# A grouped convolution as products over summed weights: a stage's products issued between the next stage's sums

## The chip, the cores and the metric

The kernel runs on one core of a Trainium2 chip. The metric is the device time of one execution in microseconds. The kernel before took 949.01 us, the median of 3 runs (947.08 to 950.08).

## The reference

The input x has 2 samples of 512 channels by 256 positions. Four residual layers follow each other, each on a layer-normalised x: a block-sparse causal convolution, a mixture of experts, an attention, and the mixture of experts again. The change touches the convolution alone:

```
xb = x.reshape(batch, n_block_row, bs, t)                # 8 blocks of 64 channels
x_unfold = xb[:, cols].reshape(batch, n_blocks * bs, t)   # 128 weight blocks choose an input block
W = block_values.reshape(n_blocks * bs, bs, ks)           # 64 x 64 weights, 16 taps each
o = conv_general_dilated(x_unfold, W, (1,), [(ks - 1, 0)], feature_group_count=n_blocks)
y = zeros(...).at[:, rows].add(o)                         # and an output block
```

Columns and rows are drawn from 0 to 3 here (block_values was made for 256 channels), while x has 8 blocks.

## The kernel before

Weight blocks with the same pair of input block (column) and output block (row) act on the same data, so the kernel first **sums** them into 64 pair sums and then makes the **products** of the sums with the input. Two taps make a stage, eight stages (0 to 7) make the 16 taps.

For stages 0 to 4 (`NPE = 5`) TensorE makes the sums: the 128 weight blocks lie on the partitions, `onehot` (128 by 64) marks each block's pair, and 8 matmuls of 64 columns (line 481) fill a PSUM **bank**; a stage has 8 banks, and 4 banks are used in turn. ScalarE copies each bank, rounded, into `cv_ws_hi` (line 245), and VectorE writes the remainder into `cv_ws_lo` (line 334). A bank can be summed anew when the remainder of the bank four before is written. For stages 5 to 7 (`ND = 3`) VectorE makes the sums itself: 16 chunks `cv_shared` of 8 weight blocks each, fetched by GpSimd's queue (line 308, three buffers, called raw_d), are added block by block into `cv_acc` (line 360, 16 additions a chunk, whose places come from registers that `load_pairs` fills). When all 16 chunks are in, `cv_acc` is split for each of these stages in four pieces (lines 254 and 343).

The input is normalised into xn, which lies in the first part of the same buffer as raw_d, and is split into `cv_xc_hi` (line 237, ScalarE) and `cv_xc_lo` (line 384, VectorE), four pairs of operations each. The products of a stage are 24 matmuls of 512 columns (line 490: 8 pairs of blocks by hi*hi, hi*lo, lo*hi), which accumulate in four other banks over all stages. Other pairs are skipped by a branch. After a stage's products a tiny matmul on zeros (line 506) frees one of the two slots of split weights (`ws_free`).

The order on every engine is written out by hand, and each engine takes its instructions in that order. On TensorE: sums 0, sums 1, then products 0, sums 2, products 1, sums 3, products 2, sums 4, and products 3 to 7. The sync engine's queue fetches the weights of the sums in chunks of 1 MB (two banks each, three buffers) and, after the first three chunks, the input. What follows the convolution starts from its last products and is unchanged.

Of the kernel before, what the change touches and what calls it, by code (L numbers as in the profile page):

```python
# [146 lines left out]
def conv_phase(nc, cm, pm, ps, ins, following, prefetch):  # L147


    with ExitStack() as ctx:  # L150
# [7 lines left out]
        raw_d = [shared[:, i * DB * DROW:(i + 1) * DB * DROW].rearrange("p (n f) -> p n f", n=DB) for i in range(3)]  # L158
# [20 lines left out]
            "x_in", "zeros_ready", "ones_ready", "cr_in", "line_in", "iota_done", "const_done",  # L179
# [4 lines left out]
        raw_in = [cm(f"cv_raw_in{i}") for i in range(3)]  # L184
        raw_d_in = [cm(f"cv_raw_d_in{i}") for i in range(3)]
# [9 lines left out]
        ZEROED = 8  # L195
        PW = NW // PIECES
# [11 lines left out]
        def _(sp):  # L208
# [12 lines left out]
            sp.dma_start(line[:, 1, :], ins["rows"].rearrange("(a n) -> a n", a=1)).then_inc(s["line_in"], 16)  # L221
            blocks_first(2)
            sp.dma_start(X[:].rearrange("p n t -> p (n t)"), ins["x_tiles"]).then_inc(s["x_in"], 16)
# [5 lines left out]
        def _(a):  # L229
# [42 lines left out]
            round_banks(0, range(6, 7))  # L272
            round_input(1, 0)
            round_banks(0, range(7, 8))
            round_input(1, 1)
            round_banks(1)
# [6 lines left out]
        def _(g):  # L283
# [20 lines left out]
            g.wait_ge(s["xc_lo_done"], 4 * B)  # L304
            for d in range(NDC):
                if d >= 3:
                    g.wait_ge(s["added"], 2 + 2 * DB * (d - 2))
                g.dma_start(raw_d[d % 3], ins["wtaps"][d].rearrange("p (n f) -> p n f", n=DB)).then_inc(raw_d_in[d % 3], 16)
# [3 lines left out]
        def _(v):  # L312
# [49 lines left out]
            def statistics(b):  # L362
                for n in range(b * GC, (b + 1) * GC):
# [23 lines left out]
            v.wait_ge(s["x_in"], 16)  # L387
            statistics(0)
            variances(0)
            low_banks(0, range(2, 3))  # L390
            statistics(1)
            variances(1)
            low_banks(0, range(3, 4))
# [5 lines left out]
            normalize(0)  # L399
            low_banks(0, range(4, 5))  # L400
            normalize(1)
            low_banks(0, range(5, 7))
            split_input(0, 0)
            low_banks(0, range(7, 8))
            split_input(0, 1)
            low_banks(1, range(0, 1))
            split_input(1, 0)
            low_banks(1, range(1, 2))
            split_input(1, 1)
            low_banks(1, range(2, 5))  # L410
# [3 lines left out]
            pairs = load_pairs(0)  # L414
            low_banks(1, range(5, 6))
            add_blocks(0, pairs)
            low_banks(1, range(6, 7))
            pairs = load_pairs(1)
            low_banks(1, range(7, 8))
            more = load_pairs(2)  # L420
            add_blocks(1, pairs)
# [1195 lines left out]
```

## Time and profile before

| what | us |
|---|---|
| median of 3 runs | 949.01 |
| lowest and highest | 947.08 and 950.08 |
| the profiled execution | 945.27 |
| its span | 943.5 |
| its mean granted clock of TensorE, as a share of 2.4 GHz | 0.978 |
| last product of the convolution ends (idle matmuls of line 58 follow) | 147.53 |

The profile is of one execution. Its times count from the start of the span; the table's own time of that execution is 1.8 us longer than the span. The granted clock is 1.00 at 2.4 GHz and 0.50 at 1.2 GHz. An idle time in brackets stands before the instruction, with what ended it. Engines are PE (TensorE), PEld (its weight loads), DVE (VectorE), ACT (ScalarE), POOL (GpSimd) and SP (sync). Each 64-column matmul of line 481 appears as two records in the trace, so a bank is 16 records.

### The profile page before, as it was taken

How to read it: one execution, taken by the hardware profiler on the slowest of the kernel's cores; microseconds unless marked ns; L12 is line 12 of the kernel's file. 1: busy time of each engine (PE TensorE's matmuls, PEld its weight loads, DVE VectorE, ACT ScalarE, POOL GpSimd, SP SyncE). 2: the span in 40 equal slices, each digit the busy share in tenths (PEclk: the TensorE clock that was granted, in tenths of full speed). 3: DMA queues.
4: the chain of work that ended last, by engine and by line, in shares of the span. 5: the costliest groups of instructions: out<-in, count | busy, mean ns of one | idle time of the engine just before them, and what ended most of it. 6: DMA issues, size and time to landing. Idle time of an engine off the chain costs nothing. (4 is left out here: it accounts for less than half of the span.)

```text
span 943.5 us, 16979 instructions
## 1 busy us (share of the span) xinstructions
PE 918.7 (97%) x5723; PEld 800.4 (85%) x5729; DVE 540.5 (57%) x1360; ACT 439.6 (47%) x952; POOL 306.9 (33%) x282
## 2 busy tenths in 40 slices
PE   9999998999999999899999999999999999999998
PEld 7999975888888887678988997898887888888887
DVE  4788875533333335678668858866875533333334
ACT  7521252534334333466656746654762534333342
POOL 1011001265555564321212112122101265555663
PEclk9598899999999999999999999999999999999999
DMA  8699601111111110200100000000001111111111
GB/s 309 221 335 374 248 2 35 46 39 44 50 50 50 50 35 15 92 23 1 35 1 22 0 33 22 0 0 0 1 1 34 34 37 47 50 50 50 48 36 61
DMA packets 23216, 60.96 MB, mean 65 GB/s; under 512 B 3138, under 2 KB 11012, under 8 KB 20612
## 3 DMA queue, kind: packets, MB, share of 16 engines
q1 hardware_dynamic: 20868, 47.80, 15.2%
q0 software_dynamic: 2304, 12.58, 3.6%
q8 instruction: 26, 0.43, 0.2%
q14 instruction: 18, 0.15, 0.0%
HBM read 59.33 MB, written 1.05 MB: 64 GB/s over the span
## 5 line engine op out<-in xcount | busy, mean ns | idle before, releaser
L809 DVE TENSOR_TENSOR f_h<-f_scaled,bank 128x512 f32<-128x512 f32 (+1 forms) x90 | 60.8, 676 | 183.6 <-POOL f_scaled L710 183.6
L710 POOL TENSOR_TENSOR f_scaled<-f_act,f_gate_rows 128x512 f32<-128x512 f32 (+1 forms) x90 | 113.5, 1262 | 135.5 <-ACT f_act L641 135.1
L899 PE MATMUL bank<-f_xt_hi,f_w_lo 128*128 128x512 f32 (+1 forms) x400 | 157.0, 393 | 0.0
L899 PE MATMUL bank<-f_xt_hi,f_w_hi 128*128 128x512 f32 (+1 forms) x400 | 156.8, 392 | 0.0
L648 ACT ACTIVATE f_h_hi<-f_h 128x512 fp32r<-128x512 f32 (+2 forms) x102 | 63.6, 624 | 184.1 <-DVE f_h L809 184.1
L899 PE MATMUL bank<-f_xt_lo,f_w_hi 128*128 128x512 f32 (+1 forms) x400 | 123.6, 390 | 0.0
L1078 ACT ACTIVATE at_prob<-bank,at_sbias,at_qrs 128x512 f32<-128x512 f32 (+3 forms) x128 | 77.6, 616 | 85.6 <-DVE at_sbias L1248 85.6
L916 PE MATMUL bank<-f_w_lo,f_h_hi 128*128 128x256 f32 (+1 forms) x400 | 113.2, 283 | 0.0
L916 PE MATMUL bank<-f_w_hi,f_h_lo 128*128 128x256 f32 (+1 forms) x400 | 113.1, 283 | 0.0
L916 PE MATMUL bank<-f_w_hi,f_h_hi 128*128 128x256 f32 (+1 forms) x400 | 113.1, 283 | 0.0
L818 DVE TENSOR_TENSOR f_h_lo<-f_h,f_h_hi 128x512 fp32r<-128x512 f32 (+2 forms) x102 | 70.1, 688 | 73.1 <-ACT f_h_hi L648 72.8
L1147 POOL TENSOR_TENSOR at_qrs<-at_qsum,minus_half 128x4 f32<-128x4 f32 x32 | 32.7, 1022 | 208.4 <-DVE at_qsum L1204 208.4
L481 PE MATMUL bank<-cv_onehot,cv_raw 128*128 128x64 f32 x640 | 87.8, 308 | 2.9 <-DVE cv_ws_lo L334 2.6
L481 PEld LDWEIGHTS bank<-cv_onehot,cv_raw 128*128 128x128 f32 x640 | 86.9, 224 | 3.5 <-issue 2.1
L899 PEld LDWEIGHTS bank<-f_xt_lo,f_w_hi 128*128 128x128 f32 (+1 forms) x400 | 74.6, 187 | 17.1 <-DVE f_xt_lo L112 0.5
L641 ACT ACTIVATE f_act<-bank 128x512 f32<-128x512 f32 (+2 forms) x102 | 59.9, 590 | 58.8 <-PE bank L899 58.7
L899 PEld LDWEIGHTS bank<-f_xt_hi,f_w_hi 128*128 128x128 f32 (+1 forms) x400 | 75.1, 188 | 13.6 <-issue 0.4
L899 PEld LDWEIGHTS bank<-f_xt_hi,f_w_lo 128*128 128x128 f32 (+1 forms) x400 | 75.1, 188 | 13.1
L916 PEld LDWEIGHTS bank<-f_w_hi,f_h_hi 128*128 128x128 f32 (+1 forms) x400 | 76.4, 191 | 3.9
L916 PEld LDWEIGHTS bank<-f_w_hi,f_h_lo 128*128 128x128 f32 (+1 forms) x400 | 76.4, 191 | 3.6
L916 PEld LDWEIGHTS bank<-f_w_lo,f_h_hi 128*128 128x128 f32 (+1 forms) x400 | 76.4, 191 | 0.0
L697 POOL TENSOR_TENSOR f_w_lo<-f_wraw,f_w_hi 128x512 fp32r<-128x512 f32 x48 | 62.1, 1294 | 37.1 <-ACT f_w_hi L627 37.1
(185 smaller groups left out, 1996.7 us busy)
## 6 DMA issues: line engine op xcount, KB each, us to landing
cv_raw<-in_wconv SPq DMA_DIRECT2D x19, 1024.0 KB, 7.3
cv_shared<-in_wtaps POOLq DMA_DIRECT2D x16, 768.0 KB, 7.2
f_wraw<-in_w SPq DMA_DIRECT2D x44, 256.0 KB, 2.7
f_wraw<-in_w SPq DMA_DIRECT2D x44, 128.0 KB, 2.5
at_wraw<-in_wqkv SPq DMA_DIRECT2D x3, 768.0 KB, 4.3
at_oraw<-in_wo SPq DMA_DIRECT2D x4, 512.0 KB, 3.6
cv_raw<-in_wconv SPq DMA_DIRECT2D x2, 512.0 KB, 4.7
X<-in_x_tiles SPq DMA_DIRECT2D x1, 1024.0 KB, 10.7
```

The lines of the kernel that those rows point to most:

```text
L481: m = t.matmul(ps[q % BANKS][:].rearrange("p (w o) -> p w o", o=OB)[:, :, o], raw[c % 3][:, w0:w0 + P], onehot[:], start=True, stop=True)
L641: a.activation(act[half][0:rows, cols], pg[half][0:rows, cols], ACT.Silu).then_inc(s["act_done"], 1)
L648: a.activation(h_hi[slot][0:rows, cols], h_f[half][0:rows, cols], ACT.Copy).then_inc(s["h_hi_done"], 1)
L697: g.tensor_tensor(w_lo[slot][:, 0:n], raw_views(m, slot, rows)[0], w_hi[slot][:, 0:n].bitcast(F32), ALU.subtract).then_inc(s["w13_lo_done" ...
L710: g.tensor_tensor(scaled[half][:, cols], act[half][:, cols], gate_rows[:, half * HALF + cols.start:half * HALF + cols.stop], ALU.mult).the ...
L809: v.tensor_tensor(h_f[half][0:rows, cols], src[half][0:rows, cols], pu[half][0:rows, cols], ALU.mult)\
L818: v.tensor_tensor(h_lo[slot][0:rows, cols], h_f[half][0:rows, cols], h_hi[slot][0:rows, cols].bitcast(F32), ALU.subtract).then_inc(s["h_lo ...
L899: mm = t.matmul(bank[half][0:rows, :], w, x, start=q == 0, stop=q == len(steps) - 1)
L916: mm = t.matmul(bank, h[hslot][0:rows, tok], w, start=first and q == 0 and j % 2 == 0, stop=last and q == 2, skip_group_check=True)
L1078: a.activation(prob[:, sl, POFF[j]:POFF[j + 1]], ps[bank][:, col:col + n], ACT.Exp, bias=sbias[:, sl, j:j + 1], scale=qrs[:, sl, j:j + 1], ...
L1147: p.tensor_tensor(qrs[:, u % 2, :], qsum[:, u % 2, :], pm["minus_half"][:, 0:NQ], ALU.pow)\
```

## The change

On TensorE the products of stage n now stand between the banks of the sums of stage n+1. In stage 1 the first five banks stand alone; after the fifth come a wait for stage 0's splits and for all of `cv_xc_lo`, then six products behind each of banks 5 to 8 (counted from one). In stages 2 to 4 three products stand behind each bank from the second to the seventh, and six behind the eighth. Stages 4 to 7 have their products after all sums, as stages 3 to 7 had before. The flag of the branch is loaded before the sums.

On the sync engine the input is fetched in two halves, the first ahead of the third weight chunk, each with a semaphore of its own. On VectorE the first half is normalised before the statistics of the second, and the splits of the input alternate with single banks. The chunks of VectorE's own sums are spread: one behind each pair of banks from stage 1's last on, and two (14 and 15) behind all banks; `load_pairs` for these two stands behind the additions of the chunk before. The first of them is fetched without waiting for `cv_xc_lo`, into the third of the buffer that xn does not use.

The core of the diff; `sum_blocks(st)`, which was a loop over a stage's banks, is now `sum_bank(st, q)` with the same body for one bank:

```diff
-        raw_d = [shared[:, i * DB * DROW:(i + 1) * DB * DROW].rearrange("p (n f) -> p n f", n=DB) for i in range(3)]
+        raw_d = [shared[:, i * DB * DROW:(i + 1) * DB * DROW].rearrange("p (n f) -> p n f", n=DB) for i in (2, 0, 1)]
...
+            def input_half(b):
+                part = slice(b * GC, (b + 1) * GC)
+                sp.dma_start(X[:, part, :].rearrange("p n t -> p (n t)"),
+                             ins["x_tiles"][:, b * GC * D:(b + 1) * GC * D]).then_inc(x_in[b], 16)
+
+            input_half(0)
             blocks_first(2)
-            sp.dma_start(X[:].rearrange("p n t -> p (n t)"), ins["x_tiles"]).then_inc(s["x_in"], 16)
+            input_half(1)
...
-            round_banks(0, range(6, 7))
+            round_banks(0, range(6, 8))
             round_input(1, 0)
-            round_banks(0, range(7, 8))
+            round_banks(1, range(0, 1))
             round_input(1, 1)
-            round_banks(1)
+            round_banks(1, range(1, 8))
...
@@ -301,8 +309,9 @@
                 g.tensor_tensor(rstd[:, part], var_eps[:, part], pm["minus_half"][:, part], ALU.pow)\
                  .then_inc(s["rstd_ready"], 1)
             g.wait_ge(s["rstd_ready"], B)
-            g.wait_ge(s["xc_lo_done"], 4 * B)
             for d in range(NDC):
+                if d == 1:
+                    g.wait_ge(s["xc_lo_done"], 4 * B)
                 if d >= 3:
...
             def statistics(b):
+                v.wait_ge(x_in[b], 16)
...
 
             low_banks(0, range(0, 2))
-            v.wait_ge(s["x_in"], 16)
             statistics(0)
             variances(0)
-            low_banks(0, range(2, 3))
+            low_banks(0, range(2, 4))
+            normalize(0)
+            low_banks(0, range(4, 5))
             statistics(1)
             variances(1)
-            low_banks(0, range(3, 4))
+            low_banks(0, range(5, 6))
             v.wait_ge(s["line_in"], 32)
             v.tensor_copy(line_f[:], line[:]).then_inc(s["cr_conv"], 1)
             v.wait_ge(s["cr_conv"], 3)
             v.scalar_tensor_tensor(out=line_pair[:], in0=line_f[:, 0, :], scalar=float(NCB), in1=line_f[:, 1, :],
                                    op0=ALU.mult, op1=ALU.add).then_inc(s["cr_conv"], 1)
-            normalize(0)
-            low_banks(0, range(4, 5))
             normalize(1)
-            low_banks(0, range(5, 7))
-            split_input(0, 0)
-            low_banks(0, range(7, 8))
-            split_input(0, 1)
-            low_banks(1, range(0, 1))
-            split_input(1, 0)
-            low_banks(1, range(1, 2))
-            split_input(1, 1)
-            low_banks(1, range(2, 5))
+            low_banks(0, range(6, 8))
+            for q in range(4):
+                split_input(q // 2, q % 2)
+                low_banks(1, range(q, q + 1))
             v.sem_inc(s["added"], 2)
             v.wait_ge(s["cr_conv"], 4)
             v.wait_ge(s["acc_zeroed"], ZEROED)
             pairs = load_pairs(0)
+            low_banks(1, range(4, 5))
+            add_blocks(0, pairs)
             low_banks(1, range(5, 6))
-            add_blocks(0, pairs)
+            pairs = load_pairs(1)
             low_banks(1, range(6, 7))
-            pairs = load_pairs(1)
+            add_blocks(1, pairs)
             low_banks(1, range(7, 8))
-            more = load_pairs(2)
-            add_blocks(1, pairs)
-            add_blocks(2, more)
-            d = 3
             for st in range(2, NPE):
-                for q in range(0, SB, 2):
-                    if d == NDC:
-                        low_banks(st, range(q, q + 2))
-                        continue
-                    low_banks(st, range(q, q + 1))
+                for i in range(4):
+                    d = 4 * (st - 2) + i + 2
+                    low_banks(st, range(2 * i, 2 * i + 1))
                     pairs = load_pairs(d)
-                    low_banks(st, range(q + 1, q + 2))
-                    if q == SB - 2 and d + 1 < NDC:
-                        more = load_pairs(d + 1)
-                        add_blocks(d, pairs)
-                        d += 1
-                        pairs = more
+                    low_banks(st, range(2 * i + 1, 2 * i + 2))
                     add_blocks(d, pairs)
-                    d += 1
+            for d in range(4 * (NPE - 2) + 2, NDC):
+                add_blocks(d, load_pairs(d))
...
-            def convolve(st):
-                t.wait_ge(s["ws_lo_done"], splits_before(st + 1) if st < NPE else splits_before(st) + PIECES // 2)
-                for c in range(NCB // 2):
-                    for r in range(GC // 2):
-                        products(st % 2, c, r, st * 2)
+            def finish_products(st):
                 t.wait_ge(s["ws_lo_done"], splits_before(st + 1))
                 high_products(st)
                 t.matmul(ps[4][:, 0:1], zeros[:, 0:P], zeros[:, 0:1], start=False, stop=False)\
...
+            def convolve(st):
+                t.wait_ge(s["ws_lo_done"], splits_before(st + 1) if st < NPE else splits_before(st) + PIECES // 2)
+                for c, r in LOW_PAIRS:
+                    products(st % 2, c, r, st * 2)
+                finish_products(st)
+
+            def sum_and_convolve(st, first):
+                n = 0
+                for q in range(SB):
+                    sum_bank(st, q)
+                    if q == first:
+                        t.wait_ge(s["ws_lo_done"], splits_before(st))
+                        t.wait_ge(s["xc_lo_done"], 4 * B)
+                    if q >= first:
+                        end = len(LOW_PAIRS) * (q - first + 1) // (SB - first)
+                        for c, r in LOW_PAIRS[n:end]:
+                            products((st - 1) % 2, c, r, (st - 1) * 2)
+                        n = end
+                finish_products(st - 1)
...
-            sum_blocks(0)
-            sum_blocks(1)
             flag = t.value_load(any_high[0:1, 0:1], min_val=0, max_val=1)
-            t.wait_ge(s["xc_lo_done"], 4 * B)
-            for st in range(NPE - 2):
-                convolve(st)
-                sum_blocks(st + 2)
-            for st in range(NPE - 2, NST - 1):
+            for q in range(SB):
+                sum_bank(0, q)
+            sum_and_convolve(1, 4)
+            for st in range(2, NPE):
+                sum_and_convolve(st, 1)
+            for st in range(NPE - 1, NST - 1):
                 convolve(st)
             convolve_last(NST - 1)
```

The start of TensorE's products, before: the rows follow 16 banks of sums (`cv_onehot` is the mark of the pairs, `cv_raw` the weights).

```order
L481 MATMUL bank<-cv_onehot,cv_raw 128x64 x128
L524 TENSOR_LOAD cv_any_high
L524 ISA x2
L490 MATMUL bank<-cv_xc_hi,cv_ws_hi 128x512
L490 MATMUL bank<-cv_xc_hi,cv_ws_lo 128x512
L490 MATMUL bank<-cv_xc_lo,cv_ws_hi 128x512
L490 MATMUL bank<-cv_xc_hi,cv_ws_hi 128x512
```

The same place now, up to the first bank behind products:

```order
L476 MATMUL bank<-cv_onehot,cv_raw 128x64 x104
L485 MATMUL bank<-cv_xc_hi,cv_ws_hi 128x512
L485 MATMUL bank<-cv_xc_hi,cv_ws_lo 128x512
L485 MATMUL bank<-cv_xc_lo,cv_ws_hi 128x512
L485 MATMUL bank<-cv_xc_hi,cv_ws_hi 128x512
L485 MATMUL bank<-cv_xc_hi,cv_ws_lo 128x512
L485 MATMUL bank<-cv_xc_lo,cv_ws_hi 128x512
L476 MATMUL bank<-cv_onehot,cv_raw 128x64 x8
```

The first products stand behind 13 banks instead of 16, ahead of the last three banks of stage 1.

TensorE where stage 2 begins, now (`zeros` is the tiny matmul that frees the slot of stage 0):

```order
L497 MATMUL bank<-zeros 128x1
L476 MATMUL bank<-cv_onehot,cv_raw 128x64 x16
L485 MATMUL bank<-cv_xc_hi,cv_ws_hi 128x512
L485 MATMUL bank<-cv_xc_hi,cv_ws_lo 128x512
L485 MATMUL bank<-cv_xc_lo,cv_ws_hi 128x512
L476 MATMUL bank<-cv_onehot,cv_raw 128x64 x8
```

Before, all 64 sums of stage 2 stood here in one row; now eight sums and three products alternate.

VectorE from the first two banks on, before (`cv_shared` written is xn):

```order
L334 TENSOR_TENSOR cv_ws_lo<-bank,cv_ws_hi 128x64x8 x2
L364 BN_STATS cv_stats<-X 128x6 x4
L369 BN_AGGR cv_moments<-cv_stats 128x2 x4
L372 TENSOR_SCALAR cv_var_eps<-cv_moments 128x4
L334 TENSOR_TENSOR cv_ws_lo<-bank,cv_ws_hi 128x64x8
L364 BN_STATS cv_stats<-X 128x6 x4
L369 BN_AGGR cv_moments<-cv_stats 128x2 x4
L372 TENSOR_SCALAR cv_var_eps<-cv_moments 128x4
L334 TENSOR_TENSOR cv_ws_lo<-bank,cv_ws_hi 128x64x8
L395 CAST cv_line_f<-cv_line 1x256
L397 SCALAR_TENSOR_TENSOR cv_line_pair<-cv_line_f 1x128
L377 TENSOR_SCALAR cv_shared<-X,cv_moments,cv_rstd 128x256 x4
```

And now:

```order
L343 TENSOR_TENSOR cv_ws_lo<-bank,cv_ws_hi 128x64x8 x2
L374 BN_STATS cv_stats<-X 128x6 x4
L379 BN_AGGR cv_moments<-cv_stats 128x2 x4
L382 TENSOR_SCALAR cv_var_eps<-cv_moments 128x4
L343 TENSOR_TENSOR cv_ws_lo<-bank,cv_ws_hi 128x64x8 x2
L387 TENSOR_SCALAR cv_shared<-X,cv_moments,cv_rstd 128x256 x4
L343 TENSOR_TENSOR cv_ws_lo<-bank,cv_ws_hi 128x64x8
L374 BN_STATS cv_stats<-X 128x6 x4
L379 BN_AGGR cv_moments<-cv_stats 128x2 x4
```

The first normalisation has moved ahead of the second half's statistics.

VectorE at the end of its own sums, before:

```order
L360 ISA
L360 TENSOR_TENSOR cv_acc<-cv_acc,cv_shared 128x96
L334 TENSOR_TENSOR cv_ws_lo<-bank,cv_ws_hi 128x64x8 x2
L343 TENSOR_TENSOR cv_ws_lo<-cv_acc,cv_ws_hi 128x1024 x12
```

And now, at the first of the two late chunks and at the end:

```order
L369 ISA
L369 TENSOR_TENSOR cv_acc<-cv_acc,cv_shared 128x96
L358 TENSOR_LOAD cv_line_pair
L369 ISA
L369 TENSOR_TENSOR cv_acc<-cv_acc,cv_shared 128x96
```

```order
L369 TENSOR_TENSOR cv_acc<-cv_acc,cv_shared 128x96
L369 ISA
L369 TENSOR_TENSOR cv_acc<-cv_acc,cv_shared 128x96
L352 TENSOR_TENSOR cv_ws_lo<-cv_acc,cv_ws_hi 128x1024 x12
```

The last chunks (a register load, then 16 additions) have moved behind the last bank's split.

## Rows read from the trace of the kernel before

**Rows 1.** The page, busy time of each engine over the span.
```profile
PE 918.7 (97%) x5723; PEld 800.4 (85%) x5729; DVE 540.5 (57%) x1360; ACT 439.6 (47%) x952; POOL 306.9 (33%) x282
```

**Rows 2.** Busy us of PE, PEld, DVE, ACT, POOL by stretch; PEclk, DMA share, GB/s.
```profile
28.00:48.00 20.00, 20.00 (x94) 20.00 (x95) 16.67 (x29) 7.75 (x12) 1.83 (x3) 0.50 0.62 225
48.00:51.00 3.00, 3.00 (x10) 2.52 (x10) 2.73 (x11) 0.60 (x1) 0.54 (x1) 0.50 1.00 416
...
86.00:99.00 13.00, 13.00 (x55) 12.42 (x56) 12.67 (x53) 2.39 (x4) 1.61 (x3) 0.50 0.94 359
```

**Rows 3.** Waits of TensorE from 0 to 150 us: total, times, longest.
```profile
PE bank L481 <- DVE cv_ws_lo L334: 2.6, 3, 1.0
...
PE bank L517 <- DVE cv_ws_lo L343: 0.7, 1, 0.7
```

**Rows 4.** Timeline of TensorE: start us, us, instruction, in brackets idle before.
```profile
7.66 10.83 PE L481 MATMUL bank<-cv_onehot,cv_raw 128*128 128x64 f32 x96
...
27.93 20.72 PE L481 MATMUL bank<-cv_onehot,cv_raw 128*128 128x64 f32 x96 [0.87 <-DVE cv_ws_lo L334]
48.40 0.77 PE L490 MATMUL bank<-cv_xc_hi,cv_ws_hi 128*128 128x512 f32 x1
...
51.49 0.39 PE L490 MATMUL bank<-cv_xc_hi,cv_ws_lo 128*128 128x512 f32 x1
...
55.49 14.48 PE L481 MATMUL bank<-cv_onehot,cv_raw 128*128 128x64 f32 x128
69.78 0.48 PE L490 MATMUL bank<-cv_xc_hi,cv_ws_hi 128*128 128x512 f32 x1
70.10 0.40 PE L490 MATMUL bank<-cv_xc_hi,cv_ws_lo 128*128 128x512 f32 x1
...
75.53 7.34 PE L481 MATMUL bank<-cv_onehot,cv_raw 128*128 128x64 f32 x64
83.88 12.35 PE L481 MATMUL bank<-cv_onehot,cv_raw 128*128 128x64 f32 x64 [1.01 <-DVE cv_ws_lo L334]
...
123.20 0.47 PE L490 MATMUL bank<-cv_xc_hi,cv_ws_hi 128*128 128x512 f32 x1
...
128.92 0.48 PE L490 MATMUL bank<-cv_xc_hi,cv_ws_hi 128*128 128x512 f32 x1
...
147.53 1.89 PE L58 MATMUL bank<-zeros 128*128 128x512 bf16 x8
```

**Rows 5.** Timeline of VectorE, with the same columns.
```profile
12.14 0.69 DVE L334 TENSOR_TENSOR cv_ws_lo<-bank,cv_ws_hi 128x512 fp32r<-128x512 f32 x1 [1.17 <-ACT cv_ws_hi L245]
14.90 1.41 DVE L364 BATCH_NORM_STATS2 cv_stats<-X 128x6 f32<-128x256 f32 x4 [2.06 <-DMA X<-in_x_tiles]
...
20.20 1.36 DVE L377 TENSOR_SCALAR cv_shared<-X,cv_moments,cv_rstd 128x256 f32<-128x256 f32 x4
...
30.91 2.48 DVE L384 TENSOR_TENSOR cv_xc_lo<-cv_shared,cv_xc_hi 64x1024 fp32r<-64x1024 f32 x2
...
37.24 2.48 DVE L384 TENSOR_TENSOR cv_xc_lo<-cv_shared,cv_xc_hi 64x1024 fp32r<-64x1024 f32 x2
...
75.20 3.23 DVE L360 TENSOR_TENSOR cv_acc<-cv_acc,cv_shared 128x96 f32 x16 [1.30 <-DMA cv_shared<-in_wtaps]
...
117.13 3.22 DVE L360 TENSOR_TENSOR cv_acc<-cv_acc,cv_shared 128x96 f32 x16
...
124.47 4.63 DVE L343 TENSOR_TENSOR cv_ws_lo<-cv_acc,cv_ws_hi 128x1024 fp32r<-128x1024 f32 x4 [2.91 <-ACT cv_ws_hi L254]
```

**Rows 6.** Timeline of ScalarE, with the same columns.
```profile
15.22 0.61 ACT L245 ACTIVATE cv_ws_hi<-bank 128x512 fp32r<-128x512 f32 x1
...
21.66 2.14 ACT L237 ACTIVATE cv_xc_hi<-cv_shared 64x1024 fp32r<-64x1024 f32 x2 [3.97 <-DVE cv_shared L377]
...
123.37 3.91 ACT L254 ACTIVATE cv_ws_hi<-cv_acc 128x1024 fp32r<-128x1024 f32 x4 [5.10 <-PE bank L506]
```

**Rows 7.** Register loads of line 349: ns min/median/max, first and last start.
```profile
L349 DVEq TENSOR_LOAD <-cv_line_pair x16: 593/598/854, 39.3 to 115.8; - x16
```

More of the change, by code:

```diff
@@ L178, in conv_phase @@
         s = {n: cm(f"cv_{n}") for n in (
-            "x_in", "zeros_ready", "ones_ready", "cr_in", "line_in", "iota_done", "const_done",
+            "zeros_ready", "ones_ready", "cr_in", "line_in", "iota_done", "const_done",
             "cr_conv", "pair_part", "pair_ready", "onehot_ready", "acc_zeroed", "added",
@@ L184, in conv_phase @@
         raw_in = [cm(f"cv_raw_in{i}") for i in range(3)]
+        x_in = [cm(f"cv_x_in{b}") for b in range(B)]
         raw_d_in = [cm(f"cv_raw_d_in{i}") for i in range(3)]
@@ L195, in conv_phase @@
         ZEROED = 8
+        LOW_PAIRS = [(c, r) for c in range(NCB // 2) for r in range(GC // 2)]
         PW = NW // PIECES
@@ L468, in _, with sum_bank @@
             t.sem_inc(s["ws_free"], 2)
-            def sum_blocks(st):
-                for q in range(SB):
-                    c, part = st * (BS // CO) + q // CB, q % CB
-                    if c > 0 and part == 0:
-                        t.wait_ge(raw_in[c % 3], 16 * (c // 3 + (c % 3 > 0)))
-                    if st * SB + q >= BANKS:
-                        t.wait_ge(s["ws_lo_done"], st * SB + q - BANKS + 1)
-                    if c == 0:
-                        t.wait_ge(first_in[part], 16)
-                    for o in range(OB):
-                        w0 = (part * OB + o) * P
-                        m = t.matmul(ps[q % BANKS][:].rearrange("p (w o) -> p w o", o=OB)[:, :, o],
-                                     raw[c % 3][:, w0:w0 + P], onehot[:], start=True, stop=True)
-                    m.then_inc(s["summed"], 1)
+            def sum_bank(st, q):
+                c, part = st * (BS // CO) + q // CB, q % CB
+                if c > 0 and part == 0:
+                    t.wait_ge(raw_in[c % 3], 16 * (c // 3 + (c % 3 > 0)))
+                if st * SB + q >= BANKS:
+                    t.wait_ge(s["ws_lo_done"], st * SB + q - BANKS + 1)
+                if c == 0:
+                    t.wait_ge(first_in[part], 16)
+                for o in range(OB):
+                    w0 = (part * OB + o) * P
+                    m = t.matmul(ps[q % BANKS][:].rearrange("p (w o) -> p w o", o=OB)[:, :, o],
+                                 raw[c % 3][:, w0:w0 + P], onehot[:], start=True, stop=True)
+                m.then_inc(s["summed"], 1)
             def products(slot, c, r, tap):
```

## The prediction

> **What bounds the kernel now.** The page comes first: TensorE is busy 97% of the span [rows 1], so a change inside the convolution must shorten TensorE's own time there, or lengthen it. Then TensorE's waits: the sums wait 2.6 us in three pieces for VectorE's splits, and the last stage 0.7 us [rows 3]. That is little. The stretches with the granted clock say more [rows 2]: from 28 to 48 us and from 86 to 99 us TensorE is full and has 0.50 of its clock, so it works at 1.2 GHz. In the timeline each of these stretches begins at a wait (0.87 us ahead of 27.93, 1.01 us ahead of 83.88) and consists of sums. At full clock a stage's 8 banks take 55.49 to 69.78, 14.3 us or 1.79 a bank; from 27.93 the 6 banks to 48.40 take 3.41 each [rows 4]. The clock came back only while products ran: half clock in all of 48 to 51 [rows 2], and the product at 51.49 has the 0.39 us of full clock [rows 4]; it never came back in 20 us of sums. So before, TensorE loses some 10 + 7 us to the half clock and 3 us to waits.
>
> The convolution ends at 147.53 [rows 4]; what follows is the same in both kernels. So I forecast how far that end moves.
>
> **The change part by part.** *1. When the products can begin.* They need all of `cv_xc_lo`, whose last split ends at 37.24 + 2.48 = 39.7 [rows 5]. The new order on VectorE, from 12.8 (its second bank, 12.14 + 0.69, is done): first the statistics, 1.41 (14.90), and aggregation and variance, 0.4, if the first half of x has landed. The whole x had landed at 14.90 [rows 5], behind two more transfers; half of it, ahead of the third chunk, should be in by 12.8. So 14.6; one bank to 15.2; the bank of ScalarE that ends at 15.22 + 0.61 [rows 6] gives 16.4; a normalisation of 1.3 (20.20, less overlap) [rows 5] 17.7; a bank 18.3; statistics 20.1; then a bank that stands on ScalarE behind a pair of copies of 2.1 (21.66) and its own 0.6 [rows 6], 21.1; the two small line operations 0.5; normalisation 22.9; two banks 24.2. Then four pairs of splits with banks between them, 3.17 a turn (30.91 to 37.24 are two turns) [rows 5]: 24.2 + 3 x 3.17 + 2.5 = 36.2. That is 3.5 us earlier than before. If x's first half lands as late as the whole did, it is 38.3; that is the late bound.
>
> *2. TensorE up to there.* 13 banks from 7.66 [rows 4] at 1.79 are done at 31. Now TensorE meets the wait for `cv_xc_lo` behind the fifth bank of stage 1. Banks 6 to 8 and all later sums are queued behind it, and so ScalarE's and VectorE's banks are too. It stands still for 5 us, to 36.2. Before, it used these microseconds for sums, but at half clock: at 36.2 it was 8.27 / 3.41 = 2.4 banks beyond the ten it had at 27.93, so 12.4. So the wait costs no lead. After it three banks and 24 products are left in stage 1: 3 x 1.79 + 5.7 (69.78 to 75.53) = 11.1 us at full clock [rows 4]. The clock will have fallen in the wait. I take 3.1 us of half-speed products, as from 48.40 to 51.49 [rows 4], and because products come in sixes with sums of 3.4 us between, twice that for the bad end. A half-speed stretch loses half its length: 1.6 (0 to 3.4). Stage 2 begins at 36.2 + 11.1 + 1.6 = 48.9, before at 55.49: **6.6 us ahead**.
>
> *3. Stages 2 to 4.* A stage of sums and products took 55.49 to 75.53 = 20.0 us [rows 4]. Three of them woven: 48.9 + 60.1 = 109.0. Before, the same state (sums 4 and products 3 done) was reached at 123.20: 14.2 ahead. The difference to the 6.6 is the half clock and the wait from 82.9 to 99, which I expect to vanish. There a pair of banks took TensorE 3.6 us, while VectorE needed two splits and a chunk of additions, 1.3 + 3.2 = 4.5 [rows 5]; it fell behind and TensorE waited. Woven, a pair takes 3.6 + 6 x 0.24 = 5.0, more than 4.5. The cover of the 4.5 is thus 0.5 us a pair and the slack of four banks.
>
> Each woven bank is a change from sums to products. The first product after sums has 0.48 us against 0.40 of the next [rows 4]. 21 such changes more would cost 1.8. But the 20.0 of the stage hold everything, and 128 records of 0.112 and 24 products of 0.233 already make 19.9. So I take 0 and keep 1.8 as a bound.
> The Trainium skill (TensorE: Matmul & The Clock Gate, What happens when you issue a matmul) says that the queue pulls weight loads ahead of running matmuls; by that the change of kind costs nothing and the sum stays, by the 0.08 row it would be 1.8 us later.
>
> *4. VectorE's own sums.* This is what eats the gain. Chunks 14 and 15 stand behind the last bank's split, and chunk 13 too has to wait for that split. The last bank's sums end 1.4 us (six products) ahead of 109.0; ScalarE and VectorE need 1.3 more: 108.9. Three chunks of 3.15 (117.13 and its like [rows 5]) and two register loads of 0.6 [rows 7], which stand between the chunks and of which I count 0.5 as seen (0 to 0.6), give **119.4**. Before, the additions ended at 117.13 + 3.22 = 120.35 [rows 5], with TensorE still busy elsewhere. So 14 us of lead on TensorE stand against 1 us on VectorE. Products 4 end at 109.0 + 5.7 = 114.7. Products 5 need half of ScalarE's and VectorE's split of `cv_acc`: 123.37 to 124.47 + 2.3 [rows 5, 6], 3.4 us, so they begin at 122.8. TensorE idles 8.1 us, a new wait. Before, they began at 128.92: 6.1 ahead.
>
> *5. The end.* The clock falls in that wait. As above, 3.1 us of products at half speed lose 1.6 (1.0 to 2.6): **4.5 ahead**. The rest keeps its distances: a slot is freed at the end of products 5, ScalarE and VectorE split the last stage, and the last stage's 0.7 us wait [rows 3] stays. End at 147.5 - 4.5 = 143.0.
>
> *6. Edits with no price.* The flag is loaded under the zero matmuls ahead of 7.66 (at most 0.5, in front of a 5 us wait). One more transfer is issued on the sync queue, far ahead of need. The first chunk of VectorE is fetched some 15 us earlier than its use. Without these covers each is under 1 us.
>
> The sum is made against the profiled 945.27 (span 943.5): 945.3 - 4.5 = 940.8. On the median of the runs, 949.01, I set the same 4.5: **944.5**.
>
> **The rivals.** *A, slower: the woven stretch stays at half clock.* If the clock falls in the 5 us wait and a mix with 1.3 us of products behind 3.4 us of sums does not raise it, then TensorE takes 40 us instead of 20 for each woven stage: 965 with one such stage, over 1000 with three. It is slower than before by more than 0.3% from some 15 us of extra half clock on. For it: sums alone kept half clock for 20 us. Against: stage 1 has six products in a row, 2.6 us at half speed, nearly the 3 that sufficed at 48.4 [rows 2]. The Trainium skill (same page, the HAM clock gate) says that "the default state is throttled, and activity releases the throttle"; a mix is less activity than pure products, which is what this rival needs. Chance 0.07.
>
> *B, the sums of VectorE end later: no measurable change.* A chunk that lands late, as at 75.20 (1.3 us) [rows 5], now delays a bank and, at the end, everything. The woven stages move 4 MB of weights and 3.1 MB of chunks in 20 us, 367 GB/s; the transfers reached 416 where they were dense, and 359 in the slow stretch [rows 2]. With the changes of kind (1.8) or one or two such delays, or a second spell of half clock (1.7), the lead of 4.5 shrinks to 0.5 to 2.8: 946.2 to 948.5. Chance 0.21, and 0.05 that nothing is won.
>
> *C, more is won.* If the clock comes back at once at both waits, 3 us are added; if the register loads hide, another 1: 940 to 941.8. Its chance is 0.13, also because the usual run is 3.7 us longer than the profiled one, and I don't know where: if by half clock in the convolution, the change removes it.
>
> *D, the change does not do what it says*: the weave would have to be undone by waits. TensorE takes its instructions in the written order, so I give it nothing of its own.
>
> **How the numbers follow.** The forecast (chance 0.54) has its own range of 942 to 946.2: 944.5 with 1.7 less loss, or with 1.7 more. Forecast and C give faster by over 0.3% (2.8 us, about what a measurement can tell from no change), 0.67. B gives within 0.3%, 0.26, A slower, 0.07. The range for 8 in 10 is 940.5 to 949.0: it leaves out A, the outer part of C and the worst of B.
>
> **What would show it.** Right: an idle of about 5 us on TensorE behind the first 13 banks, with `cv_xc_lo` as its releaser; the clock at 1.00 from some 45 to 115 us; woven stages of 20 us; an idle of about 8 us ahead of products 5, released by the splits of `cv_acc`; the last 32 additions behind the last bank. Wrong: 0.50 in woven stages (A), waits of TensorE for `cv_ws_lo` or of VectorE for `cv_shared` inside them (B), stages of over 20.5 us (the change of kind), or an end of the convolution before 141 (C).

## The result, and the profile after

The changed kernel took **942.68 us** (median of 6 runs, 941.76 to 944.21), the kernel before beside it 949.52 (6 runs, 947.08 to 952.29): a ratio of 0.993, with a 95% interval of 0.9911 to 0.995. It is faster by 6.8 us; forecast were 4.5, and a range of 940.5 to 949.0. The profiled executions differ by less: 945.27 before, 942.88 now. This difference of 2.4 us is what the rows below explain; why the medians differ by 6.8 is a matter of its own, for the first and the fourth experiment.

The page: busy time and the granted clock in 40 slices.

```profile
PE 907.2 (96%) x5729; PEld 787.6 (84%) x5729; DVE 541.1 (58%) x1360; ACT 439.6 (47%) x952; POOL 307.3 (33%) x282
...
PEclk9799979999999999999999999999999999999999
```

TensorE's busy time fell from 918.7 [rows 1] to 907.2, that is by 11.5 us; but its idle time (span less busy time) rose from 24.8 to 33.9 us, by 9.1. What is left is the 2.4 us. TensorE's waits in the first 150 us, as [rows 3] of before:

```profile
PE bank L485 <- DVE cv_ws_lo L352: 8.7, 1, 8.7
PE bank L485 <- DVE cv_xc_lo L394: 3.0, 1, 3.0
...
PE bank L476 <- DMA cv_raw<-in_wconv: 1.0, 1, 1.0
```

The 2.6 us for the splits of banks are gone. New are 3.0 us for the input, 1.0 us for a weight chunk, and **8.7 us** for the splits of `cv_acc` (line 352 there is line 343 before). Busy time by stretch, as [rows 2] (PEclk, DMA share and GB/s last):

```profile
31.00:36.00 5.00, 2.57 (x13) 2.38 (x12) 4.88 (x5) 0.60 (x1) 0.00 (x0) 0.50 0.63 226
36.00:42.00 6.00, 5.41 (x24) 4.82 (x25) 4.88 (x19) 0.18 (x1) 1.62 (x3) 0.62 0.68 239
...
50.00:70.00 20.00, 20.00 (x155) 18.72 (x154) 15.31 (x60) 4.79 (x8) 1.92 (x4) 1.00 0.91 327
70.00:90.00 20.00, 20.00 (x155) 18.74 (x155) 17.73 (x73) 4.78 (x8) 2.16 (x4) 1.00 0.95 356
90.00:110.00 20.00, 20.00 (x153) 18.68 (x153) 17.81 (x73) 4.79 (x8) 2.16 (x4) 1.00 0.83 295
...
116.00:122.00 6.00, 0.00 (x0) 0.00 (x0) 4.23 (x21) 1.30 (x2) 0.00 (x0) 0.75 0.00 0
122.00:130.00 8.00, 5.79 (x15) 4.60 (x16) 8.00 (x8) 6.39 (x7) 0.00 (x0) 0.54 0.01 2
```

The clock is full in all three woven stages, where it was 0.50 from 86 to 99 [rows 2]. In the convolution it is half only around the new waits. TensorE's timeline, answering to [rows 4]:

```profile
30.08 3.50 PE L476 MATMUL bank<-cv_onehot,cv_raw 128*128 128x64 f32 x16 [1.04 <-DMA cv_raw<-in_wconv]
36.59 0.77 PE L485 MATMUL bank<-cv_xc_hi,cv_ws_hi 128*128 128x512 f32 x1 [3.01 <-DVE cv_xc_lo L394]
...
39.28 2.50 PE L476 MATMUL bank<-cv_onehot,cv_raw 128*128 128x64 f32 x16
...
49.47 3.76 PE L476 MATMUL bank<-cv_onehot,cv_raw 128*128 128x64 f32 x32
...
53.82 1.90 PE L476 MATMUL bank<-cv_onehot,cv_raw 128*128 128x64 f32 x16
...
56.33 1.89 PE L476 MATMUL bank<-cv_onehot,cv_raw 128*128 128x64 f32 x16
...
109.52 0.18 PE L497 MATMUL bank<-zeros 128*128 128x1 bf16 x1
...
115.33 0.18 PE L497 MATMUL bank<-zeros 128*128 128x1 bf16 x1
124.21 0.79 PE L485 MATMUL bank<-cv_xc_hi,cv_ws_hi 128*128 128x512 f32 x1 [8.70 <-DVE cv_ws_lo L352]
...
129.06 0.50 PE L485 MATMUL bank<-cv_xc_lo,cv_ws_hi 128*128 128x512 f32 x1
...
132.21 0.18 PE L497 MATMUL bank<-zeros 128*128 128x1 bf16 x1
...
145.09 1.89 PE L58 MATMUL bank<-zeros 128*128 128x512 bf16 x8
```

Stage 2 begins at 49.47 (55.49 before), products 4 behind the zero matmul at 109.52 (123.20), products 5 at 124.21 (128.92), and the convolution ends at 145.09 (147.53). The lead is 6.0, 13.6, 4.7 and 2.4 us: 6.0 of it is there when stage 2 begins, 7.6 more come in the three woven stages, and most is given back behind them. VectorE and ScalarE at that place, as [rows 5] and [rows 6]:

```profile
109.48 3.23 DVE L369 TENSOR_TENSOR cv_acc<-cv_acc,cv_shared 128x96 f32 x16
113.30 0.83 DVE L369 TENSOR_TENSOR cv_acc<-cv_acc,cv_shared 128x96 f32 x4 [0.59 <-DVE cv_acc L369]
114.36 2.44 DVE L369 TENSOR_TENSOR cv_acc<-cv_acc,cv_shared 128x96 f32 x12 [0.24 <-DVE cv_acc L369]
117.38 3.23 DVE L369 TENSOR_TENSOR cv_acc<-cv_acc,cv_shared 128x96 f32 x16 [0.58 <-DVE cv_acc L369]
121.79 9.17 DVE L352 TENSOR_TENSOR cv_ws_lo<-cv_acc,cv_ws_hi 128x1024 fp32r<-128x1024 f32 x8 [1.18 <-ACT cv_ws_hi L262]
```

```profile
120.70 7.68 ACT L262 ACTIVATE cv_ws_hi<-cv_acc 128x1024 fp32r<-128x1024 f32 x8 [11.86 <-DVE cv_acc L369]
```

48 additions stand behind the last bank, with 0.59 and 0.58 us of idle ahead of the two late chunks, and end at 117.38 + 3.23 = 120.6. Before they ended at 120.35. So VectorE's own sums end no earlier than before, and all that TensorE gained up to 109.5 waits for them.

### The profile page after: what moved, and what is told of

Its sections match the earlier page's. It is cut to its first block and busy times, and to the rows that moved or that the text cites. A ratio compares the mean times of both kernels' runs of the same rounds, so it can differ in the third digit from the quotient of the medians.

```text
span 941.1 us, 16988 instructions
## 1 busy us (share of the span) xinstructions
PE 907.2 (96%) x5729; PEld 787.6 (84%) x5729; DVE 541.1 (58%) x1360; ACT 439.6 (47%) x952; POOL 307.3 (33%) x282
## 5 line engine op out<-in xcount | busy, mean ns | idle before, releaser
L476 PEld LDWEIGHTS bank<-cv_onehot,cv_raw 128*128 128x128 f32 x640 | 77.3, 196 | 3.5 <-DMA cv_raw<-in_wconv 1.2
L476 PE MATMUL bank<-cv_onehot,cv_raw 128*128 128x64 f32 x640 | 76.8, 278 | 1.0 <-DMA cv_raw<-in_wconv 1.0
```

The costliest lines, as they stand in the source:

```text
L476: m = t.matmul(ps[q % BANKS][:].rearrange("p (w o) -> p w o", o=OB)[:, :, o], raw[c % 3][:, w0:w0 + P], onehot[:], start=True, stop=True)
```

## The experiments

The granted clocks named here are means over the whole span. Beside each time stand its lowest and highest run.

**The kernel before, once more.** No edit.

> The kernel before, unchanged, to see where its usual 949.5 us stand against the 945.3 us of the profiled execution. Theory: the 4 us are half clock of TensorE in the convolution, which varies from execution to execution; then the granted clock over the span is lower in longer executions: 945.3 us had 0.978, and 4 us more of half-clock loss are 8 us more of half clock, so 0.970 at 949.5 us. Rival: the 4 us lie elsewhere (transfers, the later layers); then the clock stays at 0.978 whatever the time.

948.04 us (12 runs, 942.07 to 951.1), beside 949.28 for the same kernel in 34 further runs (941.86 to 952.39). Time and clock go together: 942.1 us at 0.981, 945.9 at 0.977, 948.3 at 0.972, 950.5 at 0.970. From 0.981 to 0.970 half clock costs 0.011 of 945 us = 10 us, and the time differs by 8.5. The theory holds: the kernel before varies by how long TensorE has half clock, and its profiled 945.27 (0.978) was a short one. Where a usual execution, at 0.972, has its further half clock no profile shows; both profiled ones have 0.978. The profile of this run has the second spell in another stage. One row of TensorE's timeline, and its page:

```profile
104.67 13.08 PE L481 MATMUL bank<-cv_onehot,cv_raw 128*128 128x64 f32 x64 [1.44 <-DVE cv_ws_lo L334]
```

```profile
PEclk9599799999999999999999999999999999999999
```

Here the 1.44 us wait is in stage 4 instead of stage 3 (1.01 us ahead of 83.88 [rows 4]), and the half clock lasts from 105 to 123.

**The weave alone**: the TensorE part of the diff on the kernel before, nothing else.

```diff
 kernel before, TensorE only:
-            sum_blocks(0)
-            sum_blocks(1)
...
+            for q in range(SB):
+                sum_bank(0, q)
+            sum_and_convolve(1, 4)
...
+            for st in range(2, NPE):
+                sum_and_convolve(st, 1)
```

> Only TensorE's order is changed (products between the banks of the next stage); the loads, the input's preparation and VectorE's own sums are ordered as before. Theory (the weave keeps the clock up, and the end of VectorE's own sums sets the end): the input is ready at 39.7 us instead of 36.5, TensorE waits longer for it, no half clock later on; the additions then end near 118 to 120 us as five chunks stand in stages 2 and 3, products 5 begin near 121 to 123 us, 941 to 945 us in all. Rival (the gain is the earlier input): no gain over before, 948 to 951 us.

946.54 us (10 runs, 943.19 to 949.72), ratio 0.9972 (0.9946 to 0.9998). The median is 1.5 us above the expected range, and the reason given for it is wrong. Its profile has half clock from 21 to 45 and again from 106 to 124, behind a 1.20 us wait for a split in woven stage 4: half clock did come later on.

**All but the weave**: the changed kernel with TensorE's order of before.

```diff
 changed kernel, TensorE only:
+            sum_blocks(0)
+            sum_blocks(1)
...
-            for q in range(SB):
-                sum_bank(0, q)
-            sum_and_convolve(1, 4)
-            for st in range(2, NPE):
-                sum_and_convolve(st, 1)
-            for st in range(NPE - 1, NST - 1):
...
+            for st in range(NPE - 2):
+                convolve(st)
+                sum_blocks(st + 2)
+            for st in range(NPE - 2, NST - 1):
```

> All of the change except TensorE's order, which is that of before (all sums of a stage, then products). Theory: half clock returns in stretches of sums, TensorE is late as before, 946 to 950 us, with the granted clock over the span back at 0.97 to 0.98. Rival (the gain is the earlier input and the spread additions): 942 to 944 us.

944.18 us (10 runs, 936.96 to 948.23), ratio 0.9952 (0.9923 to 0.998), clock 0.980 to 0.991. It lies between the two expectations, nearer to the rival's: **most of the 6.8 us come without the weave**. The profiled execution, the shortest (936.96), had no half clock between 42 and 113 us. Its page, its waits, and TensorE where stage 2 and products 4 begin:

```profile
PEclk9999989999999999999999999999999999999999
```

```profile
PE bank L486 <- DVE cv_ws_lo L352: 7.2, 1, 7.2
...
PE bank L477 <- DVE cv_ws_lo L343: 1.2, 1, 1.2
```

```profile
45.02 14.48 PE L477 MATMUL bank<-cv_onehot,cv_raw 128*128 128x64 f32 x128
...
105.29 0.18 PE L502 MATMUL bank<-zeros 128*128 128x1 bf16 x1
```

The wait ahead of products 5 is there too, 7.2 us: it belongs to the order of VectorE's additions. Stage 2 begins at 45.02, some 4.5 us earlier than in the woven kernel, which stands still behind its thirteenth bank until the input is split, and is at half clock around that wait. The three stages then take 60.3 us at full clock (45.02 to 105.29), against 60.05 woven: where the clock is full, the weave in itself saves nothing to speak of.

**The input's order alone**: that kernel, with VectorE's additions too in the order of before.

```diff
 the kernel above, VectorE only:
-            pairs = load_pairs(0)
             low_banks(1, range(4, 5))
-            add_blocks(0, pairs)
+            pairs = load_pairs(0)
             low_banks(1, range(5, 6))
-            pairs = load_pairs(1)
+            add_blocks(0, pairs)
...
-            for d in range(4 * (NPE - 2) + 2, NDC):
-                add_blocks(d, load_pairs(d))
```

> The kernel before with only the first part of the change: the input in two halves, its normalisation and splits in the new order, the first chunk of VectorE's own sums fetched early. TensorE's order and the order of VectorE's own additions are those of before. All of the change but TensorE's order took 944.2 us against 949.3. Theory A (the input's order takes away the first spell of half clock, 24 us long): granted clock 0.98 or more in most executions, 944 to 945 us, and the spread additions give little. Theory B (the spread additions take away the second spell): clock as before, 0.970 to 0.975, 948 to 949 us.

939.79 us (8 runs, 936.52 to 945.25), ratio 0.9911 (0.9884 to 0.9937), clock 0.979 to 0.987. Theory A is right in its main point, the higher clock, and too low in its size: this part of the change, alone, is worth 9 us. The clock before was 0.969 to 0.981. The first spell of half clock is shortened and not taken away: the profiled execution (940.04) has it from 30 to 48 instead of 27 to 51, 17.1 us instead of 23.9, and again from 102 to 116 behind a wait of 0.79 us. The other profiles say the same. The three with the old input order (the kernel before, twice, and the weave alone) each have 23.9 us of half clock before stage 2 begins; the nine with the new order and no zero matmuls ahead of the first products have 3.4 to 17.1 us.

**Five, five and four chunks**: one chunk instead of three behind the last bank.

```diff
 changed kernel, VectorE only:
+            d = 2
             for st in range(2, NPE):
                 for i in range(4):
-                    d = 4 * (st - 2) + i + 2
...
+                    if i == 3 and st < NPE - 1:
+                        more = load_pairs(d + 1)
+                        add_blocks(d, pairs)
+                        d += 1
+                        pairs = more
                     add_blocks(d, pairs)
+                    d += 1
-            for d in range(4 * (NPE - 2) + 2, NDC):
-                add_blocks(d, load_pairs(d))
```

> The changed kernel, but VectorE adds five of its own chunks in stages 2 and 3 and four in stage 4 (two in a row behind the last pair of banks of stages 2 and 3), so that one chunk instead of three follows the last bank. Theory (the end of VectorE's own sums sets the end): the additions end near 113 us instead of 120.6, the 8.7 us wait ahead of products 5 falls to 1 to 2 us, with little or no half clock behind it: 8 to 9 us faster, 933.5 to 935 us, unless the double chunks make TensorE wait up to 1 us in stages 2 and 3. Rival (TensorE's sums or the transfers are the bound): the wait only moves, 940 to 943 us.

938.66 us (9 runs, 934.87 to 947.78), ratio 0.9919 (0.9882 to 0.9956). The shortest execution, 934.87 at 0.996, is the one expected; most are not. The profiled one, 943.68, shows why. TensorE's timeline in woven stage 4 and two stretches:

```profile
95.78 1.89 PE L481 MATMUL bank<-cv_onehot,cv_raw 128*128 128x64 f32 x16
...
99.94 2.67 PE L481 MATMUL bank<-cv_onehot,cv_raw 128*128 128x64 f32 x16 [1.52 <-DVE cv_ws_lo L343]
...
103.79 3.51 PE L481 MATMUL bank<-cv_onehot,cv_raw 128*128 128x64 f32 x16
...
108.49 3.51 PE L481 MATMUL bank<-cv_onehot,cv_raw 128*128 128x64 f32 x16
...
113.18 3.51 PE L481 MATMUL bank<-cv_onehot,cv_raw 128*128 128x64 f32 x16
```

```profile
80.00:100.00 20.00, 18.48 (x140) 16.90 (x138) 17.78 (x75) 4.78 (x8) 2.66 (x5) 1.00 1.01 404
102.00:119.00 17.00, 17.00 (x66) 15.38 (x65) 12.64 (x52) 2.39 (x4) 0.54 (x1) 0.50 0.24 83
```

VectorE came late, TensorE waited 1.52 us, and the clock fell. From then a woven bank takes 3.51 us instead of 1.90 (the duration of its 16 records). The clock stays at half over the rest of stage 4, where three products stand behind each bank and six behind the last, until only products follow. So the mechanism of rival A of the prediction is real; the changed kernel's profiled executions have no wait in a woven stage. VectorE itself had been kept waiting by its chunks, 404 GB/s being moved from 80 to 100 us:

```profile
DVE cv_acc L369 <- DMA cv_shared<-in_wtaps: 2.1, 3, 1.0
```

**Sixes instead of threes** in these stages, on top of the kernel above.

```diff
-                        end = len(LOW_PAIRS) * (q - first + 1) // (SB - first)
+                        end = len(LOW_PAIRS) * (q - first + 1) // (SB - first) if st == 1 else q // 2 * 2 + 2 if q % 2 else n
```

> The kernel with five, five and four chunks of VectorE's own sums in stages 2 to 4, but in these stages six products stand behind every second bank instead of three behind each. Its profile with threes showed half clock from 101 to 122 us, begun by a 1.5 us wait and held by the woven stretch until the pure products. Theory (threes with sums between them don't raise the clock, sixes do, as in stage 1 of the changed kernel): a wait costs a spell of 4 to 10 us instead of 20, the slow executions near 944 to 948 us vanish, median 936 to 938 us. Rival (any mixture with sums holds the half clock): spells of 20 us as with threes, median 938.7 us or more.

939.89 us (4 runs, 937.61 to 941.15): not faster than with threes, though its runs lie closer. In its profile a wait of 1.8 us in stage 4 did not make the clock fall, so no spell began there in which sixes could have raised it, and whether sixes raise the clock in those stages stays open. In stage 1, where six products stand behind a bank in this kernel and in the changed one alike, they did not always do it at once: products began here at 35.67, and a whole bank and six more products ran at half clock before it rose at 45.

```profile
38.36 3.51 PE L481 MATMUL bank<-cv_onehot,cv_raw 128*128 128x64 f32 x16
...
44.34 2.24 PE L481 MATMUL bank<-cv_onehot,cv_raw 128*128 128x64 f32 x16
```

In the changed kernel the first bank behind six products took 2.50 us (39.28), and the clock was full from 41 us on.

**Zero matmuls in the wait ahead of products 5.**

```diff
             for st in range(NPE - 1, NST - 1):
+                if st == NPE:
+                    keep_busy(t, pm, ps[1], 36)
                 convolve(st)
```

> The changed kernel with 36 more matmuls on zeros (512 columns, 0.22 us each, 7.8 us) on TensorE between products 4 and products 5, where it idles 8.7 us. Theory (the half clock behind that wait costs time): the clock stays at 1.00 into products 5, which then take 5.7 us instead of 8.0, and since the last stage's split waits for their end, the whole is 2.3 us shorter: 940.4 us. Rival (the wait alone counts, VectorE's splits set the end): no change, 942.7 us.

941.18 us (5 runs, 938.57 to 941.5), 1.5 us less than the changed kernel, where 2.3 were expected; all five are below the changed kernel's shortest, 941.74. The profile, of the shortest run, has half clock only from 32 to 39 in the convolution, and the convolution ends at 141.73. Products 5 took 5.7 us (123.23 to 128.94), as expected, where they had taken 8.0. The idle that was 8.7 us:

```profile
PE bank L485 <- DVE cv_ws_lo L352: 0.9, 1, 0.9
```

The half clock behind the wait did cost time, if somewhat less.

**The third chunk in stage 1.** Two chunks instead of three behind the last bank.

```diff
 changed kernel, VectorE only:
             add_blocks(1, pairs)
+            pairs = load_pairs(2)
             low_banks(1, range(7, 8))
+            add_blocks(2, pairs)
...
-                    d = 4 * (st - 2) + i + 2
+                    d = 4 * (st - 2) + i + 3
...
+                    if d == NDC - 2:
+                        more = load_pairs(d + 1)
                     add_blocks(d, pairs)
-            for d in range(4 * (NPE - 2) + 2, NDC):
-                add_blocks(d, load_pairs(d))
+            add_blocks(NDC - 1, more)
```

> The changed kernel with the third chunk of VectorE's own sums moved into the idle time of stage 1, so that two chunks instead of three stand behind the last bank, and with the registers of the last chunk loaded ahead. Theory (the end of VectorE's own sums sets the end): the additions end 3.2 us and up to 1.2 us earlier, near 116.5 us instead of 120.6; the wait ahead of products 5 falls from 8.7 to 4.5 us; 938.5 us. Rival (a third chunk in stage 1 delays the splits of banks, TensorE waits in stage 2 and falls to half clock): 943 us or more, with waits for the splits inside stage 2.

938.44 us (4 runs, 937.82 to 938.97), ratio 0.9892 (0.9858 to 0.9927). This is the number expected, and the wait too:

```profile
PE bank L488 <- DVE cv_ws_lo L352: 4.6, 1, 4.6
```

4.1 us less of the wait are 4.2 us less of the whole. So in the changed kernel the end of VectorE's own sums does set when the convolution ends.

**Woven, with the old additions.** The changed kernel, VectorE's additions as before (the edit of the fourth experiment).

> The changed kernel (woven, new input order) with VectorE's own additions in the order of before: three chunks in stage 1, five in stages 2 and 3, three in stage 4, none behind the last bank. It completes the square: with the new input order, unwoven and old additions took 939.8 us, unwoven and spread 944.2, woven and spread 942.7. Theory (the spread additions cost the gain by their late end, the weave gains only where no wait falls into it): the additions end near 110 us, no wait ahead of products 5, but VectorE's double chunks in stages 2 and 3 make TensorE wait and fall to half clock in woven stretches in some executions: 936 to 942 us with a wide spread. Rival (the weave itself is what costs): 943 us or more.

936.62 us (4 runs, 934.35 to 943.1), ratio 0.9886 (0.9836 to 0.9935). Two runs of four are at 934.4 and 935.0 with a clock of 0.995; the profiled one, 943.10, had a 1.24 us wait in woven stage 4 and half clock from 103 to 121. It is the same picture as with five, five and four.

**The changed kernel, once more.** No edit.

> The changed kernel once more, beside the others of this call, to have its time on the same chip: 942 to 943 us, with a spread under 3 us, as its half clock lies in the same two places in every execution (clock 0.986 to 0.989).

942.97 us (10 runs, 941.74 to 944.38), beside 947.97 for the kernel before, ratio 0.9953 (0.9929 to 0.9978). As expected, it hardly varies. Its profile has the same 8.7 us wait.

**The third chunk in stage 1, and zero matmuls in both waits.** On top of that kernel (`ps[4]` accumulates, so zeros add nothing):

```diff
                 for q in range(SB):
+                    if st == 1 and q == first:
+                        for _ in range(4):
+                            t.matmul(ps[4][:], zeros[:, 0:P], zeros[:], start=False, stop=False)
                     sum_bank(st, q)
+                    if st == 1 and q == first:
+                        for _ in range(17):
+                            t.matmul(ps[4][:], zeros[:, 0:P], zeros[:], start=False, stop=False)
...
+                if st == NPE:
+                    keep_busy(t, pm, ps[1], 20)
                 convolve(st)
```

> The kernel with the third chunk in stage 1 (938.4 us) and zero matmuls in TensorE's waits: 4 ahead of bank 13, 17 behind it (3.7 us, in the wait for the input's splits) and 20 (4.3 us) ahead of products 5. Theory (both waits cost half-clock time on top of themselves): clock 1.00 through the convolution, 1.5 to 2 us saved in stage 1 and 1.7 to 2.3 behind the second wait: 934.5 to 935.5 us. Rival (TensorE's lead out of stage 1 is lost again at the end of VectorE's own sums): stage 1's part is worth nothing, since those additions follow the banks it is worth the same; if they don't follow, only 1.7 to 2.3 us, 936.5 us.

**934.78 us** (6 runs, 933.97 to 935.36), ratio 0.9873 (0.9836 to 0.9909): as expected, better than both kernels, and the steadiest. The longest of its new waits, and its clock:

```profile
PE bank L488 <- DVE cv_xc_lo L394: 0.7, 1, 0.7
```

```profile
PEclk9999999999999999999999999999999999999999
```

There is no half clock in the convolution, which ends at 136.81. How the gain divides between the two fillings was not measured here.

What the input's new order is worth (9 us), and how the other two parts combine with it, medians in us:

| with the new input order | old additions | spread additions |
|---|---|---|
| TensorE as before | 939.8 | 944.2 |
| woven | 936.6 | 942.7 and 943.0 |

By the medians the spread additions cost 4 to 6 us and the weave gives 1 to 3 on either side; with the old input order it gave 2.7. These are medians of 4 to 10 runs, each measured beside the kernel before, which took from 948.0 to 949.5. Woven against unwoven the runs overlap in both columns, so the weave's own share is not settled. The runs of the two columns overlap as well; the additions' share rests on the waits of 8.7 and 7.2 us ahead of products 5 too, and in the woven row on the third-chunk run.

## Why the prediction was right, and where not

*The total.* 942.7 is within the forecast's own range as I wrote it, 942 to 946.2. By the margin that I gave for it, 1.7 us on either side of 944.5, its lower end should have read 942.8, and the result lies at that edge. That it is so near is partly luck, as two misses point opposite ways. Profile against profile the change gave 2.4 us, not 4.5, so the sum over the parts promised 2.1 too much. The other 4.4 of the 6.8 come almost wholly from the kernel before: its usual run is 4 us longer than its profiled one and has more half clock. I had this in rival C, as something not known, and set the lead of one execution on the median. That last step of the sum is the weak one; the clocks of many runs, which were not among the data then, show its size.

*1 and 2, the products' beginning.* The last split of the input ends at 36.4 (36.2 forecast). The wait is 3.0 us instead of 5, because a weight chunk held the thirteenth bank up for 1.0 us and the clock fell there already. Products begin at 36.59, stage 2 at 49.47 (48.9). Right, to 0.6 us. That the wait costs no lead holds only against the kernel before, which was at half clock there; the unwoven kernel with the new input order, at full clock, was some 4.5 us ahead of this one where stage 2 began.

*3, the woven stages.* 49.47 to 109.52 are 60.05 us, forecast 60.1. The 21 changes of kind had no price, as I took it: a woven bank is 2.49 to 2.51 us (53.82 to 56.33), and 16 x 0.112 + 3 x 0.233 make 2.49. The Trainium skill (TensorE: Matmul & The Clock Gate, What happens when you issue a matmul) says that weight loads are pulled ahead of running matmuls; the trace agrees in that a woven stage is no longer than its parts. That the second spell of half clock vanishes was right of this kernel. That the weave is what keeps the clock is not shown: the unwoven kernel with the rest of the change had no such spell in its profile either, and three woven kernels had one.

*4, VectorE's own sums.* The mechanism was right, and the run with the third chunk in stage 1 shows it. The size was small by 0.6 us: the register loads are seen with 0.59 each instead of 0.5, a chunk takes 3.23 us instead of 3.15, and one chunk has 0.24 us of idle in it, whose cause no run shows. The chunks also began 0.6 us later, as stage 2 did. The additions end at 120.6 (119.4), products 5 begin at 124.21 (122.8) behind a wait of 8.7 (8.1).

*5, the end.* Products 5 took 8.0 us (124.21 to 132.21), 2.3 more than at full clock, where I took 1.6. The 3.1 us of half-speed products that I had from 48.40 to 51.49 were 4.9 here (124.21 to 129.06, where the duration falls from 0.63 to 0.50). With the 1.4 of step 4 that makes the end 145.1 instead of 143.0.

*The rivals.* A did not happen here, but its mechanism did in three other kernels: a wait of 1.2 to 1.5 us in a woven stage, and 17 to 20 us of half clock. In their profiles it fell on one stage, and none of the three kernels had a median above that of the kernel before. Whether 0.07 was a good chance one outcome can't tell. B did not happen; its late chunks appeared as soon as the additions were denser.

*What I missed altogether* is the share of the parts. I took the input's order for a step that costs and gives nothing, since TensorE was only as far at 36.2 as before. It is worth the most when alone: with the old order TensorE is at half clock for 23.9 us before stage 2 in each of three profiles. In two of them two or three waits of 0.5 to 0.9 us for splits of banks stand ahead of it, in the third one of 1.5 us for a weight chunk. And the spread additions were not a neutral cover for the banks but, by the table, the largest loss. I saw their late end, and did not price the version without it.

## What to carry to other kernels

When an engine off the critical path does a fixed amount of work, spreading it to keep others from waiting also moves its end; look at what waits for the end before the lead elsewhere is counted. Here a wait of 0.8 to 1.5 us was several times followed by 14 to 20 us of half clock, an estimated 7 to 10 us lost (half of each spell), though not every such wait was. So look for short waits ahead of the stretches of half clock, take them away, and try matmuls on zeros in those that stay. Test the parts of a change singly: here one part gave 9 us, and the whole 7.

## What the runs showed of the hardware

With five, five and four chunks, a stretch of 64-column sums with three 512-column products behind every eight, and six behind the last, did not bring TensorE's clock back from 1.2 to 2.4 GHz in 17 us (102 to 119 us, granted 0.50). Products alone did so within 3.1 us of their start before (48.40 to 51.49 [rows 4]) and 4.9 us now (124.21 to 129.06). Sixes with sums between them took some 4 us in the changed kernel (36.59 to 41) and 9 in that of the sixes (35.67 to 45). At full clock, the mixture of sums and threes held it for 60 us in the changed kernel. A short wait stood ahead of the long spells, but did not always bring one: 1.01 us did in the kernel before (ahead of 83.88), 1.80 us in woven stage 4 of the kernel with sixes did not. The kernel before varies by 10 us from one execution to the next (941.9 to 952.4 in 34 runs), and the mean granted clock goes with it (0.981 to 0.969); with the waits filled, the spread is 1.4 us.
